# Five half pieces of landed adjacency instead of eight, five of high and low parts instead of four

## What is computed

```python
h = item_feat @ W_item.T + b_item
b = user_feat @ W_user.T + b_user            # user_feat = layernorm(x)
x = x + relu(adj @ h + b)                    # adj is 10000 x 10000
...
lstm_out = _lstm(layernorm(x)[None], W_ih, W_hh, b_ih, b_hh)
w = g * lstm_out                             # g: argmax of two logits of each row
inc = jnp.cumsum(w, axis=1)
x = x + 2.0 * lstm_out + (inc - w) * fw_att + (inc[:, -1:, :] - inc) * bw_att
```

## Time and profile before

| | us |
|---|---|
| median of 3 runs | 1427.13 (1426.66 to 1427.23) |
| the profiled execution | 1430.41 |
| its span, first to last instruction | 1428.6 |
| TensorE busy in the span | 1405.4 (98%) |
| VectorE busy | 1272.8 (89%) |
| ScalarE busy | 1055.8 (74%) |
| the adjacency stage, block 0 to the last matmul of block 19 | about 1118 |
| one block, blocks 2 to 18 | 54.6 |

### The profile page before, as it was taken

One profiled execution on the slowest core, in us unless ns is written; L12 is line 12 of the kernel. 1 busy time (PEld: TensorE's weight loads), 2 busy tenths in 40 slices (PEclk: granted clock), 3 DMA queues, 4 the chain that ended last, 5 costly groups with the idle time before them and its releaser, 6 DMA issues.

```text
span 1428.6 us, 26247 instructions
## 1 busy us (share of the span) xinstructions
PE 1405.4 (98%) x7464; PEld 1215.2 (85%) x7464; DVE 1272.8 (89%) x2102; ACT 1055.8 (74%) x1449; POOL 210.0 (15%) x189
## 2 busy tenths in 40 slices
PE   9999999999999999999999999999999999999995
PEld 8878888888888888888888888888888899999994
DVE  7999999999999999999999999999999766676666
ACT  6677787787777777877887877877877676556663
POOL 0000100000000000001001001001000131037775
PEclk9999999999999999999999999999999999999997
DMA  9999999999999999999999999999999203000003
GB/s 375 354 346 379 403 389 387 399 391 374 404 391 382 403 387 381 401 388 398 384 392 392 397 381 402 390 381 401 391 379 386 102 0 144 0 1 1 0 0 144
DMA packets 143466, 442.96 MB, mean 310 GB/s; under 512 B 23944, under 2 KB 43337, under 8 KB 143307
## 3 DMA queue, kind: packets, MB, share of 16 engines
q1 hardware_dynamic: 126048, 426.43, 77.1%
q10 hardware_dynamic: 17387, 16.14, 3.9%
HBM read 432.15 MB, written 10.36 MB: 310 GB/s over the span
## 4 chain that ended last, share of the span: by engine, by line
PE 94%; DVE 5%; ACT 0%; issue 0%; POOL 0%; DVEq 0%; ACTq 0%; POOLq 0%
PE psG L884 24%; PE psG L885 24%; PE psG L886 24%; PE psZ L989 10%; PE psZ L977 3%; PE psZ L975 3%; PE psZ L979 3%; DVE a_lo L1210 2%; PE psZ L995 1%; PE psT L859 1%; PE psI L932 1%; DVE u L1525 1%; DVE item_lo L1243 0%; DVE u L1224 0%; PE psV L938 0%; PE psG L877 0%
## 5 line engine op out<-in xcount | busy, mean ns | idle before, releaser
L667 ACT ACTIVATE a_hi<-raw 128x1000 fp32r<-128x1000 f32 (+1 forms) x800 | 819.1, 1030 | 240.4 <-PE psG L886 222.5
L1210 DVE TENSOR_TENSOR a_lo<-raw,a_hi 128x1000 fp32r<-128x1000 f32 (+1 forms) x800 | 897.0, 1170 | 19.3 <-ACT a_hi L667 14.7
L884 PE MATMUL psG<-a_hi,item_hi 128*128 128x500 f32 x1560 | 610.3, 391 | 1.4 <-DVE a_lo L1210 1.4
L885 PE MATMUL psG<-a_lo,item_hi 128*128 128x500 f32 x1560 | 605.5, 388 | 0.0
L886 PE MATMUL psG<-a_hi,item_lo 128*128 128x500 f32 x1560 | 604.1, 387 | 0.0
L884 PEld LDWEIGHTS psG<-a_hi,item_hi 128*128 128x128 f32 x1560 | 293.2, 188 | 63.3 <-DVE a_lo L1210 2.4
L886 PEld LDWEIGHTS psG<-a_hi,item_lo 128*128 128x128 f32 x1560 | 292.8, 188 | 59.4
L885 PEld LDWEIGHTS psG<-a_lo,item_hi 128*128 128x128 f32 x1560 | 293.3, 188 | 55.5
L989 PE MATMUL psZ<-hist,wh 128*128 (+1 forms) x1264 | 167.9, 276 | 2.9 <-DVE hist L1363 2.2
L989 PEld LDWEIGHTS psZ<-hist,wh 128*128 128x128 f32 x1264 | 154.7, 192 | 3.8 <-issue 2.4
L468 POOL TENSOR_TENSOR row_terms<-var,minus_half 125x4 f32<-125x4 f32 x20 | 37.6, 1879 | 679.8 <-DVE var L1161 679.8
(11 more groups left out here) (188 smaller groups left out, 865.4 us busy)
## 6 DMA issues: line engine op xcount, KB each, us to landing
raw<-in_adj_main SPq DMA_DIRECT2D x760, 500.0 KB, 6.7
raw<-in_adj_main SPq DMA_DIRECT2D x40, 250.0 KB, 5.5
sq<-rstd_copy ACTq DMA_DIRECT2D x20, 250.0 KB, 6.7
u<-x_copy SPq DMA_DIRECT2D x1, 5000.0 KB, 14.5
x_copy<-x_rows SPq DMA_DIRECT2D x19, 250.0 KB, 7.2
sq<-rows_copy ACTq DMA_DIRECT2D x19, 250.0 KB, 6.1
un_bb<-rows_copy ACTq DMA_DIRECT2D x19, 250.0 KB, 7.6
u<-in_itemT SPq DMA_DIRECT2D x9, 512.0 KB, 9.4
```

The costliest lines, as they stand in the source:

```text
L667: nc.scalar.activation(a_hi[:, s % CUT, 0:n], raw[:, r % RAW, at:at + n], ACT.Copy)\
L884: pe.matmul(bank, w_hi, hi, start=(c == 0), stop=False)
L885: pe.matmul(bank, w_hi, lo, start=False, stop=False)
L1210: last = dve.tensor_tensor(a_lo[:, s % CUT, 0:m], raw[:, r % RAW, at:at + m], a_hi[:, s % CUT, 0:m].bitcast(f32), ALU.subtract)
```

## The change

The two constants become RAW = 5 and CUT = 5, and `raw` is laid out in half pieces, as the other two rings are: half s of a block lies in slot `s % 5` of all three. In bytes per partition `raw` goes from 32000 to 20000, and `a_hi` and `a_lo` from 16000 to 20000 each. There are five landing semaphores instead of eight. SP waits, before it loads half s, for the low part of half s - 5 instead of s - 8 (the text of the wait was `2 * (r - RAW) + h + 1`); ScalarE waits, before it makes the high part of half s, for TensorE's half s - 5 instead of s - 4. A few small tensors are allocated at other places. No instruction that computes or moves data is added, removed or reordered.

```diff
-RAW = 4
-CUT = 4
+RAW = 5
+CUT = 5
...
-assert PIECES % RAW == 0 and HALVES % CUT == 0 and SIZES[LAST] < MAXC == 2 * HALF
+assert HALVES % RAW == 0 and HALVES % CUT == 0 and SIZES[LAST] < MAXC == 2 * HALF
...
-        raw = sb("raw", [P, RAW, MAXC * BW], f32, first)
+        raw = sb("raw", [P, RAW, HALF * BW], f32, first)
...
-        raw_in = [sem(f"raw_in{s}") for s in range(2 * RAW)]
+        raw_in = [sem(f"raw_in{s}") for s in range(RAW)]
...
             def load_block(j, wait=True, move=True, prefetch=True, items={}):
                 for r in range(PIECES):
                     for h in range(2):
-                        landed = raw_in[2 * (r % RAW) + h]
+                        s = 2 * r + h
+                        landed = raw_in[s % RAW]
                         n, at = half_cols(r, h)
                         n -= BW * (r == LAST and h == 1)
-                        if wait or r >= RAW:
-                            sp.wait_ge(lo_ready, HALVES * j + 2 * (r - RAW) + h + 1)
-                        sp.dma_start(raw[:, r % RAW, at:at + n],
+                        if wait or s >= RAW:
+                            sp.wait_ge(lo_ready, HALVES * j + s - RAW + 1)
+                        sp.dma_start(raw[:, s % RAW, 0:n],
                                      adj_main[j, :, STARTS[r] * BW + at:STARTS[r] * BW + at + n]).then_inc(landed, 16)
...
             def split_hi(j, r, h, wait=True):
                 s = 2 * r + h
                 n, at = half_cols(r, h)
-                tails = len(STACK) if h == 1 else 0
-                per_block = PIECES // RAW + tails * (r % RAW == LAST % RAW)
-                act.wait_ge(raw_in[2 * (r % RAW) + h], 16 * (per_block * j + r // RAW + 1 + tails * (r == LAST)))
+                extra = len(STACK)
+                per_block = HALVES // RAW + extra * (s % RAW == (HALVES - 1) % RAW)
+                act.wait_ge(raw_in[s % RAW], 16 * (per_block * j + s // RAW + 1 + extra * (s == HALVES - 1)))
                 if wait or s >= CUT:
                     act.wait_ge(halves_done, HALVES * j + (s - CUT + 1))
-                nc.scalar.activation(a_hi[:, s % CUT, 0:n], raw[:, r % RAW, at:at + n], ACT.Copy)\
+                nc.scalar.activation(a_hi[:, s % CUT, 0:n], raw[:, s % RAW, 0:n], ACT.Copy)\
                     .then_inc(hi_ready, 1)
...
-                last = dve.tensor_tensor(a_lo[:, s % CUT, 0:m], raw[:, r % RAW, at:at + m],
+                last = dve.tensor_tensor(a_lo[:, s % CUT, 0:m], raw[:, s % RAW, 0:m],
                                          a_hi[:, s % CUT, 0:m].bitcast(f32), ALU.subtract)
```

More of the change, by code:

```diff
@@ L151, in program @@
         item_lo = sb("item_lo", [P, (CH + 1) * HID], f32r, first)
-        raw = sb("raw", [P, RAW, MAXC * BW], f32, first)
+        raw = sb("raw", [P, RAW, HALF * BW], f32, first)
+        mean_sum = sb("mean_sum", [SW, SUB], f32, first)
+        mean_gap = sb("mean_gap", [SW, SUB], f32, first)
+        gap_sq = sb("gap_sq", [SW, SUB], f32, first)
+        spread = sb("spread", [SW, SUB], f32, first)
+        var = sb("var", [SW, SUB], f32, first)
+        rstd1 = sb("rstd1", [SW, SUB], f32, first)
+        row_terms = sb("row_terms", [SW, 2, SUB], f32, first)
         a_hi = sb("a_hi", [P, CUT, HALF * BW], f32r, first)
+        moments = sb("moments", [SW, SUB, 6], f32, first)
         a_lo = sb("a_lo", [P, CUT, HALF * BW], f32r, first)
@@ L167, in program @@
         v = un_bb[:, 0:BW]
[L168 to L174, removed]
         rstd, shift_rows = row_terms[:, 0, :], row_terms[:, 1, :]
-        rstd1 = sb("rstd1", [SW, SUB], f32, first)
         factors = sq
@@ L412, in load_block @@
                             for p0 in STACK:
-                                sp.dma_start(raw[p0:p0 + TAIL, r % RAW, at + n:at + n + BW], adj_tail[j])\
+                                sp.dma_start(raw[p0:p0 + TAIL, s % RAW, n:n + BW], adj_tail[j])\
                                     .then_inc(landed, 16)
@@ L1213, in split_lo @@
                     mid = slice(STACK[1], STACK[1] + TAIL)
-                    last = dve.tensor_tensor(a_hi[mid, s % CUT, m:n], raw[mid, r % RAW, at + m:at + n],
+                    last = dve.tensor_tensor(a_hi[mid, s % CUT, m:n], raw[mid, s % RAW, m:n],
                                              a_hi[mid, s % CUT, m:n].bitcast(f32), ALU.subtract)
```

## The result

The changed kernel takes 1687.12 us (1685.14 to 1691.4, three runs) against 1427.13: a ratio of 1.182, interval 1.181 to 1.184. It is slower by 260 us, not by the 59 that were forecast, and outside the range. Rival C had this place: it was priced at 1697 us and given one chance in ten.

The account below looks back on a forecast made before the run. TensorE was taken to bound the kernel at 54.6 us a block; the shallower landed ring would make it 57.6. Profiled 1430.4 + 57 (19 blocks) + 2 (start) + 0 = 1489.4, median 1486 us; range 1426 to 1560.

Parts of the forecast that it names:

- Rival C: Landed ring: landing stays near 6.1 us because the engines are the limit; turn 8.6 us, 1697 us; chance 0.10.
- Part 1: High and low rings, four to five: TensorE has almost no idle time to win; value 0, bounds 0 to -2.5 us.
- The turn of a slot is its transfer plus 2.5 us: Landed ring: subtraction, copy and handovers add about 2.5 us to each transfer, leaving 4.3 us of 6.82 for it.
- The transfer with five slots is 4.4 us: Landed ring: median landing taken from 66 to 82 us, bounds 3.5 and 6.1; turn 6.9 us, block 55.2 us.
- VectorE's other work adds 2.4 us a block: Adjacency blocks: a third of VectorE's 7.2 us of other work enters each block; bounds 0 and 7.2 us.
- a third of each extra: VectorE in the five-slot ring: each extra piece of work delays the turn by a third of its length.
- Lumps of other transfers: Adjacency blocks: other reads, loads and stores add no more to the forecast; 3.1 us a block kept for the upper end.
- The start costs 2 us: Block 0: SP's later issues, with the third item load behind three waits, add 2 us; bounds 0 and +8.
- Rival A: Landed ring: with a transfer of 3.5 us five slots suffice and TensorE goes on as before; 1427 us; chance 0.15.
- Rival B: Adjacency stage: the ring suffices and fifth high and low halves remove TensorE idle time, up to 2.5 us; 1422 us; chance 0.05.
- The rule of the Trainium skill: Loads of halves: fixed cost of about 2.0 us plus bytes at 436 GB/s; a half lands after about 3.2 us.

Follow-up runs that it names:

- after_halfload: The changed kernel, but from block 1 on each load brings only the first half of its columns (250 KB instead of 500): 1469.70 us, ratio 1.029.
- after_nospread: The changed kernel with the three broadcasts of a block cut to one partition, apart from the first of block 0: 1602.61 us, ratio 1.123.

## Why the prediction was wrong

- *TensorE has no wait to win, so nothing gets faster (Part 1).* Right. Nor did the fifth high and low half repay anything: 1687.1 with five, 1683.6 with four of them and the same depth of the landed ring.
- *The turn of a slot is its transfer plus 2.5 us.* Right, and the step that carried the forecast's sign: the chain shows 2.54 us in a turn without waits, the mean over 527 turns is 2.88.
- *The transfer with five slots is 4.4 us.* **This is the step that failed.** It is 5.6 us in the median and 5.67 in the mean, and (5.67 - 4.4) x 8 = 10.2 us a block is nearly all of the 10.8 by which the 68.4 us exceed the forecast 57.6. The stretch from 66 to 82 us was chosen because few halves were in flight; it also had a slower pace (262 GB/s), and only the end of its window has a broadcast:

```profile
81.71 0.33 ACTq L645 DMA_DIRECT2D sq<-rstd_copy  x1
```

All the loads of the window were issued before it. The prediction said that 4.4 was "rather low than high", and that the other transfers need not be counted, since the 4.4 had been "read with the tails and one such read beside it"; that second reading of the rows was wrong. The runs give 5.0 us for halves without broadcasts and 16-byte stores, and 115 us of the 260 to these two (1687.1 - 1572.5). The row that was near the truth, 6.1 us from 82 to 90 us, stands right behind this broadcast. It was put down to a burst that filled the queue, set as a bound of the transfer and priced as rival C, and left out of the range.
- *VectorE's other work adds 2.4 us a block.* Not far off as a sum, though not shown to be VectorE's alone: all waits inside the turn come to (2.88 - 2.5) x 8 = 3.0 us a block. Its rule, a third of each extra, did not hold for further work: six additions more cost a tenth of their length, a seventh at most.
- *Lumps of other transfers: nothing, beyond what is in the 4.4.* The same failed step seen from its other side, and no further term: (1687.1 - 1572.5) / 19 = 6.0 us a block.
- *The start costs 2 us.* 4.5 us by the traces (block 1 begins at 86.8 us instead of 82.3), within the bounds of 0 to 8.
- *Rival A* (the ring suffices below 4.0 us) is refuted by after_halfload, as far as a median goes. *Rival B* had nothing to take. *Rival C* had nearly the right time and turn (8.6 us against 8.55), in part by luck: its transfer of 6.1 us was 0.4 too long and its 2.5 us for the rest 0.4 too short. Its reason, that the engines and not the queue are the limit, is half right at most: at 312 GB/s and a share of 0.92 the engines were not at the 391 GB/s that they move with three slots more. That the number of slots limits is shown by the runs: 312 GB/s with five, 362 with six, 388 with seven, 391 with eight. Why a transfer still takes 5.0 us with nothing else beside the halves stays open.

The rule of the Trainium skill that was weighed (DMA: Bandwidth & Descriptors, section Anatomy of one DMA, SWDGE (gpsimd) path; 3.2 us as an estimate for a half of 500 KB) was farther from the 5.6 us than the rows were. No run here has a half alone in an empty queue.

## What to carry to other kernels

Before a ring is made shallower, write its turn as transfer plus hold time, and compare it with slots times pace. Take the transfer from the loaded stretches, with their peaks, and not from a light one: a queue's landing time falls less than in proportion when fewer transfers are in flight (6.7 to 5.6 us from eight slots to five), and if the row near full traffic lies above the break-even point, its price belongs inside the range. Look at what else was issued in the stretch that a row is read from. In a ring without slack, some small transfers beside the large ones are dear, broadcasts and stores in 16-byte pieces here, while a plain load of 250 KB was not: three broadcasts a block cost 85 us with five slots and nothing that one run can tell with eight.

## What was not expected of the hardware

- Two stores of 375 pieces of 16 bytes in all, 6 KB a block, cost 30 to 41 us over 19 blocks in the ring of five, a third to a half of the 85 us of the 750 KB of broadcasts.
- A load of x of 250 KB, issued by SP between the halves, cost nothing measurable (1602.6 and 1603.5 us).
- Transfers of 64 partitions moved 240 GB/s with full engines.
- TensorE's granted clock, 1.00 in the middle of the kernel before, was 0.98 in the changed kernel from 200 to 1100 us and 0.83 from 640 to 650 us, which is the mean of time at 2.4 and time at 1.2 GHz. TensorE had waited 3.4 us for a low half up to 643.87 us:

```profile
640.00:650.00 10.00, 6.58 (x22) 5.06 (x22) 6.88 (x7) 6.96 (x8) 0.00 (x0) 0.83 0.89 324
```

This is on the path. The chain that ended last, seen from 643 to 655 us, is TensorE's from 643.87 to 654.28 us, and goes on to VectorE, which waits for transposes that stand behind these matmuls:

```profile
643.87 0.49 PE psG L885
644.36 0.22 PE psG L886
...
646.34 0.41 PE psG L887
646.75 0.42 PE psG L885
...
653.83 0.45 PE psT L860 x4
```

Eight matmuls of that stretch take 0.41 to 0.42 us each instead of 0.22 to 0.23, some 1.5 us in all. From 200 to 1100 us TensorE has 55 us of the chain, and 40 matmuls in it are slow ones, which makes about 7.6 us; without the broadcasts (after_nospread) the chain has no matmul in that window and the granted clock is 1.00. So a small part of what the broadcasts cost, an estimate of some 10 us over the stage, seems to come by this way and not by the transfers themselves.
